# A four-stage transformer block on one core: the merged projection Wq^T Wk moves from a first stage of its own into the tail of the routing and the start of the experts, in plain float32

## The chip, the cores and the metric

The kernel runs on one core of a Trainium2 chip. The metric is the device time of one execution in microseconds. Engines are named as in the profile: PE is TensorE (matmuls; PEld its weight loads), DVE VectorE, ACT ScalarE, POOL GpSimd, SP SyncE, which here only issues DMA transfers. TensorE's clock has two levels, 1.2 and 2.4 GHz; the profile gives the granted share of the full one (0.50 or 1.00).

## What is computed

Batch B = 8, length L = 256, width D = 1024, so 16 row tiles of 128. Four residual stages (cut to what matters):

```python
x = x + tanh(g_xattn[0]) * autocorrelation(layernorm(x), ctx, ctx)   # lag attention: spectra by DFT matmuls, top 11 lags
x = x + tanh(g_ffn[0])   * moe(layernorm(x), gate_w, u, g, d)        # 16 experts, top 2, inner width 112
# third stage
Q = einsum('btx,dx->btd', layernorm(x), Wq) + bq
K = einsum('bpx,dx->bpd', ctx, Wk) + bk
x = x + tanh(g_xattn[1]) * softmax(Q K^T / 32) ctx
x = x + tanh(g_ffn[1])   * int8_style_ffn(layernorm(x))              # gate, up, down, hidden 512
```

Scores of the third stage are made as x (Wq^T Wk) ctx^T plus terms with the biases: `M` = Wq^T Wk is the merged projection (1024 x 1024), `shift` = Wk^T bq, `key_bias` = Wq^T bk, `constant` = bq.bk.

## The kernel before, in words

The program is a row of functions, one block of all engines each, with a barrier between two blocks: `merge_projections`, `lag_attention`, `route`, `experts`, `context_attention`, `quantised_ffn`. X, all 16 tiles, stays in SBUF. Each engine runs its instructions in the order written; semaphores tie them.

- `merge_projections` (names `mp_`): Wq and Wk arrive a 512 KB row block at a time. ACT makes the high part in F32R, DVE the low part, and PE makes M in 16 blocks of 128 x 512, 8 steps over k each, by `split_product` (three F32R matmuls, L44 to L46). M's parts go to DRAM (`merged`). X is loaded behind the weights, and `RowScale` makes the first layernorm's scale and shift for all tiles at once.
- `lag_attention` (`la_`): 16 units (batch b, half h of the width), software-pipelined over three steps. PE runs plain float32 products with the Fourier tables (`full_product`, L52; the trace shows each as two records). Each unit: spectra of v, of q, of v again, `positions` of the unit before, turned weights, `correlate`, `weight_spectra`. In the steps in which a batch ends, DVE also makes the next layernorm's statistics (`running_ln`: `BatchScale.variance` and `.tables`, with one `pow` on POOL). PE's third spectrum waits for ACT's copies (L253), which wait for DVE's `o_products` (L373).
- `route` (`rt_`): ACT normalises tile t into a ring of four (`rt_xn`, L677), SP stores it (`normal`), PE turns it (L766) and makes logits (L785), ACT and DVE copy it. ACT's write of tile t waits until the store of tile t-4 has landed. Then comes a DVE chain (top 2, counts, ranks, slots, ending with `place`, L758), with two PE sums in it (L790, L791). POOL loads M's parts (8 MB, L669) when all logits are there.
- `experts` (`ex_`): POOL writes the token lists by 32 indirect DMAs (L871), SP reads the list back, fills unused rows of `produced` with zeros (10 x 512 KB here), POOL gathers the first tile (`ex_xr`), and PE turns it (L949) and runs 39 tiles of gate/up (L963) and down (L975).
- `context_attention` (`xa_`): POOL gathers expert rows (two per tile, L1219 to L1222), DVE adds them to X (L1328), layernorm of batch 0 with POOL's `pow` (L564), then PE runs 8 `a_block`s per batch with M's two parts as stationary operands.

## Time and profile before

| | us |
|---|---|
| runs | 1636.74, 1643.25, 1646.53 |
| median | 1643.25 |
| profiled execution, its own time | 1643.94 |
| its span in the trace | 1642.2 |
| PE busy | 1346.5 (82%) |
| DVE busy | 794.9 (48%) |
| ACT busy | 534.8 (33%) |
| POOL busy | 424.0 (26%) |

Times in the rows below are microseconds from the start of the span. In a timeline row come start, duration, engine, line, operation, output<-input, count, and in brackets how long the engine was idle before it and what ended that. A row with a count above one spans several instructions.

### The profile page before, as it was taken

Reading aid. Unit: us, or ns where it says so; the run is one execution under the profiler, and the core shown is the slowest. Engines: PE = TensorE matmul, PEld = TensorE weight load, DVE = VectorE, ACT = ScalarE, POOL = GpSimd, SP = SyncE. Lnnn points to the kernel's source line nnn. Section 1 sums busy time; section 2 is a strip of 40 time slices with the busy share of each in tenths; the row PEclk is TensorE's granted clock in tenths of the full one; section 3 lists DMA queues with packets and bytes.
Section 4 is the critical chain, followed back from the end, with each engine's and each line's share of the span. In section 5 each row is a group of like instructions: output and inputs, shape, how many; then the busy total and the mean of one; then the engine's idle time right before and its main releaser. Section 6 shows DMA issues by size and latency. Waiting matters only on the chain. (4 is left out here: it accounts for less than half of the span.)

```text
span 1642.2 us, 20159 instructions
## 1 busy us (share of the span) xinstructions
PE 1346.5 (82%) x6217; PEld 914.8 (56%) x6217; DVE 794.9 (48%) x2134; ACT 534.8 (33%) x841; POOL 424.0 (26%) x501
## 2 busy tenths in 40 slices
PE   7896999999999976703888888829999999927876
PEld 6663444545445444603666666619888888714443
DVE  3163676786777763410222222234444443226896
ACT  3112322232232212301334333412222222147884
POOL 0130232232222321053111111232111110026785
PEclk9998999999999997855999998959999999968999
DMA  5742000000000002564666666443333321050111
GB/s 179 294 141 84 26 13 26 13 13 25 13 26 13 0 1 92 220 201 180 195 195 220 219 218 207 154 145 112 103 103 102 102 77 52 26 188 36 64 51 77
DMA packets 59426, 172.78 MB, mean 105 GB/s; under 512 B 7792, under 2 KB 15984, under 8 KB 59248
## 3 DMA queue, kind: packets, MB, share of 16 engines
q1 hardware_dynamic: 41152, 117.06, 20.1%
q0 software_dynamic: 18224, 55.08, 11.0%
q8 instruction: 29, 0.48, 0.1%
q14 instruction: 21, 0.17, 0.0%
HBM read 121.21 MB, written 50.90 MB: 105 GB/s over the span
## 5 line engine op out<-in xcount | busy, mean ns | idle before, releaser
L44 PE MATMUL xa_bank<-xa_xT_hi,M_hi 128*128 128x256 f32 x512 | 153.3, 299 | 0.0
L46 PE MATMUL xa_bank<-xa_xT_hi,M_lo 128*128 128x256 f32 x512 | 143.8, 281 | 0.0
L45 PE MATMUL xa_bank<-xa_xT_lo,M_hi 128*128 128x256 f32 x512 | 143.8, 281 | 0.0
L52 PE MATMUL la_bank<-la_v_raw,la_tab 128*128 128x512 f32 x256 | 118.5, 606 | 25.6 <-ACT la_v_spec L253 12.9
L963 PEld LDWEIGHTS ex_bank<-ex_gu,ex_xT 128*128 128x128 f32 x624 | 123.9, 201 | 25.6 <-issue 24.1
L963 PE MATMUL ex_bank<-ex_gu,ex_xT 128*128 128x224 f32 x624 | 132.8, 368 | 1.3 <-issue 1.3
L217 POOL TENSOR_TENSOR la_osum<-la_oprod 128x512 f32<-128x512 f32 x64 | 82.8, 1314 | 192.9 <-DVE la_oprod L373 192.9
L52 PE MATMUL la_bank<-la_osum,la_tab 128*128 128x512 f32 x256 | 116.3, 608 | 13.8 <-POOL la_osum L217 13.8
L949 PE MATMUL ex_bank<-ex_ident,ex_xr 128*128 128x128 f32 x320 | 45.5, 288 | 95.1 <-DMA ex_xr<-normal,ex_current 95.1
L52 PE MATMUL la_bank<-la_wT,la_tab 128*128 128x512 f32 x256 | 112.6, 593 | 1.2 <-ACT la_wT L274 1.2
L52 PEld LDWEIGHTS la_bank<-la_v_raw,la_tab 128*128 128x128 f32 x256 | 48.0, 193 | 92.3 <-issue 67.7
L1287 ACT ACTIVATE xa_A<-xa_bank,shift 128x256 f32<-128x256 f32 x64 | 30.3, 473 | 208.9 <-PE xa_bank L46 208.9
L975 PE MATMUL ex_bank<-ex_dn,ex_hT 112*128 112x512 f32 x156 | 86.3, 680 | 14.3 <-ACT ex_hT L913 14.3
L44 PEld LDWEIGHTS xa_bank<-xa_xT_hi,M_hi 128*128 128x128 f32 x512 | 96.5, 188 | 2.8 <-issue 1.7
L45 PEld LDWEIGHTS xa_bank<-xa_xT_lo,M_hi 128*128 128x128 f32 x512 | 96.6, 189 | 2.5 <-issue 1.7
L373 DVE TENSOR_TENSOR la_oprod<-la_bank,la_v_spec 128x512 f32<-128x512 f32 x128 | 80.1, 685 | 34.6 <-issue 23.4
L46 PEld LDWEIGHTS xa_bank<-xa_xT_hi,M_lo 128*128 128x128 f32 x512 | 96.4, 188 | 0.0
L949 PEld LDWEIGHTS ex_bank<-ex_ident,ex_xr 128*128 128x128 f32 x320 | 36.6, 145 | 104.7 <-issue 71.1
L52 PEld LDWEIGHTS la_bank<-la_osum,la_tab 128*128 128x128 f32 x256 | 49.9, 196 | 77.9 <-issue 62.4
L52 PEld LDWEIGHTS la_bank<-la_wT,la_tab 128*128 128x128 f32 x256 | 48.6, 190 | 55.8 <-issue 53.6
L940 DVE COPY ex_y<-ex_bank 128x512 f32<-128x512 f32 x39 | 27.0, 691 | 106.1 <-ACT ex_y L916 106.1
L929 DVE COPY ex_xT<-ex_bank 128x512 f32<-128x512 f32 x40 | 27.7, 691 | 96.6 <-PE ex_bank L949 96.6
(280 smaller groups left out, 2767.2 us busy)
## 6 DMA issues: line engine op xcount, KB each, us to landing
produced<-ex_y SPq DMA_DIRECT2D x39, 512.0 KB, 3.0
ex_gu<-in_gate_up SPq DMA_DIRECT2D x16, 896.0 KB, 6.2
X<-in_x SPq DMA_DIRECT2D x8, 1024.0 KB, 12.9
la_v_raw<-in_ctx SPq DMA_DIRECT2D x16, 512.0 KB, 3.8
normal<-rt_xn SPq DMA_DIRECT2D x16, 512.0 KB, 2.7
xa_fT<-in_ctx_T SPq DMA_DIRECT2D x8, 1024.0 KB, 5.6
xa_f<-in_ctx SPq DMA_DIRECT2D x8, 1024.0 KB, 5.0
result<-qf_final SPq DMA_DIRECT2D x16, 512.0 KB, 2.6
```

What stands on the lines that cost most here:

```text
L44: pe.matmul(out, a[0], b[0], start=first, stop=False)
L45: pe.matmul(out, a[0], b[1], start=False, stop=False)
L46: return pe.matmul(out, a[1], b[0], start=False, stop=last)
L52: return pe.matmul(out, a, b, start=first, stop=last)
L217: pool.tensor_tensor(osum[:, i, :], oprod[:, a, :], oprod[:, a + 1, :], ALU.add if i % 2 == 0 else ALU.subtract).then_inc(s["osums"], 1)
L373: dve.tensor_tensor(oprod[:, 2 * (i % 2) + k, :], bank[bk][:], vs[:, h, vk, :], ALU.mult).then_inc(s["oprods"], 1)
L929: dve.tensor_copy(xT[:, 4:8, :].rearrange("p a b -> p (a b)"), bank[3][:]).then_inc(s["xT_dve"], 1)
L940: dve.tensor_copy(y[:, 512:1024], bank[5][:]).then_inc(s["y_dve"], 1)
L949: m = pe.transpose(bank[2 + k // 4][:, (k % 4) * P:(k % 4 + 1) * P], xr[:, k * P:(k + 1) * P], ident[:])
L963: m = pe.matmul(bank[0][:, 0:UP_COLS], xT[:, k, :], gu[:, slot, k * UP_COLS:(k + 1) * UP_COLS], start=(k == 0), stop=(k == KD - 1))
L975: m = pe.matmul(bank[4 + i][:], hT[:], dn[:, slot, i * 512:(i + 1) * 512], start=True, stop=True)
L1287: act.activation(A[:, m % AHEAD, :], bank[2 + m % 2][:, 0:L], ACT.Identity, bias=shift[:, m:m + 1]).then_inc(s["a_out"], 1)
```

## The change

`merge_projections` is gone. `lag_attention` comes first: SP loads X batch by batch between the context loads, and DVE makes the first layernorm per batch (`BatchScale`, as for the second), batch b+2 at the end of each step with h = 1. During lag attention SP also zeroes tiles 32 to 47 of `produced` and loads Wk whole. `route` loads Wq whole after its eighth store, and PE makes M there in plain float32 by `merged_product` (8 `matmul`s of 128 x 512 a block): 4 of the 16 blocks in `route` after the logits, 12 at the start of `experts` ahead of the first turn. The bias vectors are made by DVE (`weigh`, sums weighted by the bias) and 17 PE products of one column. `context_attention` makes the parts: ACT the high one (8 copies), POOL the low one (8 subtractions between its gathers).

```diff
@@ lag_attention, SP
+            load_x(0)
             load_v(0, 0, 0)
+            sp.dma_start(tab[:], tables).then_inc(s["tab_in"], 16)
+            sp.dma_start(graw[:], column(gate, 0)).then_inc(s["gate_in"], 16)
             load_v(1, 0, 1)
-            with sp.Fori(1, B) as b:
+            load_x(1)
+            load_x(2)
...
+            with sp.Fori(1, B - 2) as b:
                 for h in range(2):
                     load_v(2 * b + h, b, h)
+                    fill(2 * b + (FEWEST - 2 + h))
+                load_x(b + 2)
+            sp.dma_start(Wk_home[:], Wk.rearrange("(k p) n -> p k n", p=P)).then_inc(s["Wk_in"], 16)
@@ lag_attention, ACT and DVE
+                act.wait_ge(norm.ready, b + 1)
...
+                if due is not None:
+                    dve.wait_ge(x_in, 16 * (due + 1))
+                    norm.variance(dve, X, due)
+                    norm.tables(dve, due)
+            dve.wait_ge(x_in, 16)
+            norm.variance(dve, X, 0)
+            norm.tables(dve, 0)
             steps(dve, step)
@@
+EARLY = 4
+SUMS_AT = 1
+def merged_product(pe, out, W, n):
+
+    for k in range(KD):
+        last = pe.matmul(out, W[1][:, k, (n // 2) * P:(n // 2 + 1) * P], W[0][:, k, (n % 2) * 512:(n % 2 + 1) * 512],
+                         start=(k == 0), stop=(k == KD - 1))
+    return last
@@ route, SP
             for t in range(TILES):
+                if t == TILES // 2:
+                    sp.dma_start(W[1][:], Wq.rearrange("(k p) n -> p k n", p=P)).then_inc(s["wq_in"], 16)
                 sp.wait_ge(s["xn_ready"], t + 1)
@@ route, POOL
-            pool.wait_ge(s["logits"], TILES)
-            for part in range(2):
-                pool.dma_start(M[part][:], merged[part].rearrange("(k p) n -> p k n", p=P)).then_inc(m_in, 16)
@@ route, DVE
             for t in range(TILES):
+                if t >= TILES - KD:
+                    weigh(0, t - (TILES - KD))
...
             dve.tensor_tensor(place[:], place[:], place_tile[:], ALU.add).then_inc(s["placed"], 1)
+            dve.wait_ge(s["wq_in"], 16)
+            for k in range(KD):
+                weigh(1, k)
+            dve.wait_ge(s["columns"], 1)
@@ route, PE
+            for n in range(EARLY):
+                if n == SUMS_AT:
+                    sums()
+                at_least(pe, s["m_out"], n - 3)
+                merged_product(pe, bank[n % 4][:], W, n).then_inc(s["m_pe"], 1)
+            pe.wait_ge(s["by_bias"], 2 * KD)
...
@@ experts, PE
+            for n in range(EARLY, 2 * KD):
+                at_least(pe, s["m_out"], n - EARLY - 3)
+                merged_product(pe, bank[merged_bank[n % 4]][:], W, n).then_inc(s["m_pe"], 1)
...
@@ experts, SP
-            with sp.Fori(total, MAX_TILES + 1) as g:
-                row = sp.snap(g * P)
-                sp.dma_start(produced[bass.ds(row, P), :], zeros[:]).then_inc(s["filled"], 16)
@@ context_attention, POOL
+            merged_low(0)
             gather(0, 2)
+            merged_low(1)
             gather(0, 3)
+            merged_low(2)
             gather(1, 0)
...
@@ context_attention, ACT
+            for m in range(KD):
+                part = (slice(None), slice(None), slice(m * P, (m + 1) * P))
+                act.activation(M[0][part], M32[part], ACT.Copy).then_inc(s["m_hi"], 1)
             act.wait_ge(s["gate_in"], 32)
```

PE, from the last logits (L785 before, L840 after) to the first turned expert tile: before.

```order
L785 MATMUL rt_bank<-rt_gw,rt_xnT 128x16 x7
L790 MATMUL rt_bank<-rt_both,rt_ones 128x256 [waits la_v_ev1]
L791 MATMUL rt_bank<-rt_both,rt_before 128x256
L605 UNCONDITIONAL_BRANCH
L942 UNCONDITIONAL_BRANCH [waits barrier_Pool_Activation_PE_DVE_SP_release]
L949 MATMUL ex_bank<-ex_ident,ex_xr 128x128 [waits la_top_chain,la_oprods]
```

The same place after the change; L602 is `merged_product`, L821 and L822 the two sums, L855 and L856 the bias columns.

```order
L840 MATMUL rt_bank<-rt_gw,rt_xnT 128x16 x7
L602 MATMUL rt_bank<-Wk,Wq 128x512 [waits la_corr_sb,la_filled,la_zeroed]
L602 MATMUL rt_bank<-Wk,Wq 128x512 x7
L821 MATMUL rt_bank<-rt_both,rt_ones 128x256 [waits la_q_ready]
L822 MATMUL rt_bank<-rt_both,rt_before 128x256
L602 MATMUL rt_bank<-Wk,Wq 128x512 x24
L855 MATMUL rt_bank<-rt_ones,rt_by_bias 128x1 [waits la_maxed,la_exed]
L855 MATMUL rt_bank<-rt_ones,rt_by_bias 128x1 x15
L856 MATMUL rt_bank<-rt_b_sum,rt_ones 128x1
L614 UNCONDITIONAL_BRANCH
L1001 UNCONDITIONAL_BRANCH [waits barrier_Pool_Activation_PE_DVE_SP_release]
L602 MATMUL ex_bank<-Wk,Wq 128x512 [waits la_achain]
```

After that last row PE has 95 more matmuls of L602 before it turns the first tile: one block stands ahead of the sums, three behind them, twelve behind the barrier. (Semaphores keep the number, and so the name, of an earlier block here.)

POOL at the start of `context_attention` after the change; L1145 is `merged_low`, L1128 to L1131 a gather, L555 the `pow` of the layernorm of batch 0.

```order
L1145 TENSOR_TENSOR M_lo<-M_2476,M_hi 128x8x128 [waits xa_m_hi]
L1128 TENSOR_TENSOR xa_small_u<-slots,xa_small_u 128x1 [waits xa_combined]
L1130 TENSOR_TENSOR xa_small_u<-xa_small_u 128x1 [waits xa_at]
L1131 DMA xa_got<-produced,xa_small_u 128x1024
...
L1145 TENSOR_TENSOR M_lo<-M_2476,M_hi 128x8x128 [waits xa_m_hi]
L555 TENSOR_TENSOR ln_small<-ln_small 128x2 [waits xa_ln_var_ready,xa_ln_power_set]
```

Before, the gathers and the `pow` followed each other with nothing between; now five of the eight subtractions stand ahead of the `pow` (the rows shown are the first subtraction, the first gather behind it, and the fifth subtraction with the `pow`; three more pairs of a subtraction and a gather lie between).

SP in `route` after the change: the weights' 4 MB stand between the eighth and the ninth store, on the same queue.

```order
L663 DMA token_of<-rt_no_token 128x50 [waits la_v_ev2]
L668 DMA normal<-rt_xn 128x1024 [waits la_dchain] x8
L666 DMA Wq<-in_Wq 128x8x1024
L668 DMA normal<-rt_xn 128x1024 [waits la_dchain] x8
L614 UNCONDITIONAL_BRANCH [waits la_out_pe,la_top_chain,la_osums,la_oprods]
```

Before, all 16 stores stood in one row (L649).

## Rows read from the trace of the kernel before

**Rows 1.** Busy time in stretches: start:end, length, busy of each engine, PEclk, DMA share, GB/s.

```profile
340.00:360.00 20.00, 20.00 (x62) 10.90 (x61) 14.44 (x48) 4.26 (x8) 4.65 (x5) 1.00 0.07 25
...
766.00:770.00 4.00, 4.00 (x11) 3.60 (x12) 0.00 (x0) 0.58 (x1) 0.17 (x1) 0.50 0.98 373
```

**Rows 2.** Timeline by engine, from the start to lag attention's first products.

```profile
0.83 0.40 SPq L1016 DMA_DIRECT2D mp_b_raw<-in_bq  x1
...
125.98 0.34 SPq L179 DMA_DIRECT2D la_tab<-in_tables  x1
...
126.05 0.07 DVE L305 MEMSET la_nextv<- 128x8 f32 x1 [0.34 <-PEq L986]
...
135.32 0.20 ACT L234 ACTIVATE la_tg<-la_graw 128x1 f32<-128x1 f32 x1 [9.82 <-DMA la_graw<-in_g_xattn]
135.43 1.50 ACT L242 ACTIVATE la_q_n<-X,first_ln_shift,first_ln_scale 128x512 f32<-128x512 f32 x2
...
142.05 3.60 PE L52 MATMUL la_bank<-la_q_n,la_tab 128*128 128x512 f32 x8
```

**Rows 3.** Timeline of DVE, lag attention, a step with a layernorm.

```profile
347.00 0.06 DVE L569 MEMSET running_ln_small<- 128x2 f32 x1
...
352.05 0.43 DVE L337 MAX8 la_top<-la_corr 128x8 f32<-128x256 f32 x1
...
357.19 2.48 DVE L373 TENSOR_TENSOR la_oprod<-la_bank,la_v_spec 128x512 f32<-128x512 f32 x4
```

**Rows 4.** Timeline of PE, lag attention, 300 to 368 us and 600 to 645 us.

```profile
305.40 3.70 PE L52 MATMUL la_bank<-la_v_raw,la_tab 128*128 128x512 f32 x8 [1.21 <-ACT la_v_spec L253]
308.94 7.03 PE L52 MATMUL la_bank<-la_osum,la_tab 128*128 128x512 f32 x16
...
334.75 3.70 PE L52 MATMUL la_bank<-la_v_raw,la_tab 128*128 128x512 f32 x8 [0.71 <-ACT la_v_spec L253]
...
625.50 8.61 PE L52 MATMUL la_bank<-la_osum,la_tab 128*128 128x512 f32 x16 [6.75 <-POOL la_osum L217]
```

**Rows 5.** Timeline of the routing, by engine.

```profile
655.58 1.23 ACT L677 ACTIVATE rt_xn<-X,running_ln_shift,running_ln_scale 128x1024 f32<-128x1024 f32 x1
...
667.05 1.23 ACT L677 ACTIVATE rt_xn<-X,running_ln_shift,running_ln_scale 128x1024 f32<-128x1024 f32 x1
...
679.93 4.35 PE L785 MATMUL rt_bank<-rt_gw,rt_xnT 128*128 128x16 f32 x34
...
704.04 0.19 DVE L758 CUSTOM_DVE_ANT_0 place<-place,rt_place_tile 128x64 uint16<-128x64 uint16 x1
...
709.47 0.20 POOL L864 MEMSET ex_ident<- 128x128 f32 x1 [22.71 <-POOLq L605]
```

**Rows 6.** DMA issues, 685 to 765 us: KB each, median us from issue to landing.

```profile
M_hi<-merged POOLq DMA_DIRECT2D x1, 4096.0 KB, 14.0
```

**Rows 7.** Timeline of the experts' start, by engine.

```profile
749.82 0.97 POOL L871 DMA_INDIRECT token_of<-token,place  x1 [0.30 <-issue]
...
762.57 1.94 PE L949 MATMUL ex_bank<-ex_ident,ex_xr 128*128 128x128 f32 x8 [70.43 <-DMA ex_xr<-normal,ex_current]
...
775.26 3.19 PE L963 MATMUL ex_bank<-ex_gu,ex_xT 128*128 128x224 f32 x16
...
781.73 3.23 PE L963 MATMUL ex_bank<-ex_gu,ex_xT 128*128 128x224 f32 x16
```

**Rows 8.** Timeline of context attention's start.

```profile
1084.92 0.19 POOL L1219 TENSOR_TENSOR xa_small_u<-slots,xa_small_u 128x1 uint32<-128x1 uint32 x1 [1.02 <-DVE X L1328]
...
1094.22 0.72 POOL L564 TENSOR_TENSOR ln_small<-ln_small 128x2 f32<-128x2 f32 x1 [1.55 <-DVE ln_small L581]
...
1102.95 2.67 DVE L1328 SCALAR_TENSOR_TENSOR X<-xa_got,weights,X 128x1024 f32<-128x1024 f32 x2
...
1104.57 1.09 POOL L1221 TENSOR_TENSOR xa_small_u<-xa_small_u 128x1 uint32<-128x1 uint32 x1
```

**Rows 9.** Groups by line of POOL, whole span: count, busy us, mean ns.

```profile
L1600 POOL TENSOR_TENSOR qf_final<-qf_y,X 128x1024 f32<-128x1024 f32 x16 | 37.7, 2354 | 11.0 <-DVE qf_y L1673 11.0
```

More of the change, by code:

```diff
@@ L167, in on @@
                     return u + off, b + (h + off) // 2, (h + off) % 2
-                step(on)
+                step(on, b + 2 if h == 1 and not (isinstance(b, int) and b + 2 >= B) else None)
             for u in range(-2, 2):
                 one(u, u // 2, u % 2)
-            with eng.Fori(1, B - 1) as b:
+            with eng.Fori(1, B - 2) as b:
                 one(2 * b, b, 0)
                 one(2 * b + 1, b, 1)
-            for u in range(U - 2, U + 1):
+            for u in range(U - 4, U + 1):
                 one(u, u // 2, u % 2)
@@ L636, in route @@
         no_token = sb("no_token", [P, ROW_TILES], I32)
-        names = "gw_in consts turned xnT_act xnT_dve logits one xn_ready chain sums_pe slots_ready ex_ready gap_ready no_token no_list placed".split()
+        b_raw = sb("b_raw", [P, 2, KD])
+        bb = sb("bb", [P, KD])
+        b_sum = sb("b_sum", [P, 1])
+        by_bias = sb("by_bias", [P, 2, D])
+        key_sum = sb("key_sum", [P, KD])
+        names = "gw_in consts turned xnT_act xnT_dve logits one xn_ready chain sums_pe slots_ready ex_ready gap_ready no_token no_list placed b_in wq_in dot by_bias columns key_sum key_hi m_pe m_out".split()
         s = {n: sem(n) for n in names}
-        stored = [sem(f"stored{i}") for i in range(4)]
+        stored = [sem(f"stored{i}") for i in range(RING)]
         block = ctx.enter_context(nc.Block())
@@ L766, in turn, with sums @@
                 return pe.transpose(bank[2 * (t % 2) + k // 4][:, (k % 4) * P:(k % 4 + 1) * P],
-                                    xn[:, t % 4, k * P:(k + 1) * P], ident[:])
+                                    xn[:, t % RING, k * P:(k + 1) * P], ident[:])
+            def sums():
+                pe.wait_ge(s["chain"], 6)
+                flat = both[:].rearrange("p t e -> p (t e)")
+                pe.matmul(bank[5][:, 0:TILES * EXPERTS], ones[:], flat, start=True, stop=True)
+                pe.matmul(bank[6][:, 0:TILES * EXPERTS], before[:], flat, start=True, stop=True).then_inc(s["sums_pe"], 1)
             for t in range(2):
@@ L787, in _, with experts @@
                 m.then_inc(s["logits"], 1)
-            pe.wait_ge(s["chain"], 6)
-            flat = both[:].rearrange("p t e -> p (t e)")
-            pe.matmul(bank[5][:, 0:TILES * EXPERTS], ones[:], flat, start=True, stop=True)
-            pe.matmul(bank[6][:, 0:TILES * EXPERTS], before[:], flat, start=True, stop=True).then_inc(s["sums_pe"], 1)
-def experts(nc, gate_up, down, normal, token_of, token, place, produced, first_tile):
+            pe.wait_ge(s["xnT_act"], TILES)
+            pe.wait_ge(s["xnT_dve"], TILES)
+            pe.wait_ge(s["wq_in"], 16)
+            for n in range(EARLY):
+                if n == SUMS_AT:
[3 more added lines that the diff above has]
+            pe.wait_ge(s["by_bias"], 2 * KD)
+            pe.wait_ge(s["dot"], 2)
+            for v in range(2):
+                for i in range(KD):
+                    pe.matmul(bank[7][:, v * KD + i:v * KD + i + 1], by_bias[:, v, i * P:(i + 1) * P], ones[:, 0:1], start=True, stop=True)
+            pe.matmul(bank[7][:, 2 * KD:2 * KD + 1], ones[:], b_sum[:], start=True, stop=True).then_inc(s["columns"], 1)
+def experts(nc, gate_up, down, normal, token_of, token, place, produced, first_tile, W, M32):
     with ExitStack() as ctx:
@@ L951, in turn @@
                         m.then_inc(s["turned"], 1)
+            for n in range(EARLY, 2 * KD):
+                at_least(pe, s["m_out"], n - EARLY - 3)
+                merged_product(pe, bank[merged_bank[n % 4]][:], W, n).then_inc(s["m_pe"], 1)
+            pe.wait_ge(s["m_out"], 2 * KD - EARLY)
             turn(0)
@@ L1136, in context_attention @@
-def context_attention(nc, produced, slots, weights, ffn_gate, features, features_T, M, m_in, shift, key_bias, constant, gate, X,
+def context_attention(nc, produced, slots, weights, ffn_gate, features, features_T, M32, M, shift, key_bias, constant, gate, X,
                       after):
@@ L1765, in build, with with_guest @@
         running = BatchScale(nc, stack, "running_ln")
[L1766 to L1775 removed]
+        with ExitStack() as projection:
+            def with_guest(name, guest):
+                at = -(-nc.sbuf_base // 32) * 32
+                owner = projection.enter_context(nc.sbuf_tensor(name, [P, KD, D], F32R))
+                return owner, nc.alloc_sbuf_tensor_at(guest, [P, KD, D], F32, offset=at)
+            M_hi, Wk_home = with_guest("M_hi", "Wk")
+            lag_attention(nc, x, ctx, g_xattn, tables, Wk, Wk_home, X, running, produced)
+            M_lo, M32 = with_guest("M_lo", "M32")
+            slots = projection.enter_context(nc.sbuf_tensor("slots", [P, TILES, 2], U32))
+            weights = projection.enter_context(nc.sbuf_tensor("weights", [P, TILES, 2], F32))
+            first_tile = projection.enter_context(nc.sbuf_tensor("first_tile", [P, EXPERTS + 1], I32))
             with ExitStack() as lists:
```

318 lines of the change are left out of this document (96 added, 222 removed).

## The prediction

> **What bounds the kernel now.** I read the stretches first. In lag attention PE is busy all 20 us of a stretch at a granted clock of 1.00 and DVE 14.4 of them [rows 1]. Then I read the timelines where PE does not work: before the first Fourier product of q at 142.05, which the merged projection and the loads of lag attention precede [rows 2], and from the end of the logits at 684.3 [rows 5] to the first turned expert tile at 762.57, where PE sat idle for 70.4 us [rows 7]. The change takes work out of the first place and puts it into the second, so the end of the kernel moves by what is saved at 142.05 less what comes later. In between, the chain is: lag attention on PE, a DVE chain in the routing, POOL's list writing, PE's experts, context attention on PE.
>
> **The start.** The work before lag attention goes. What stays is its own entry: before, the table's transfer was issued at 125.98 and the gate value, behind the table, was used at 135.32, 9.3 us later [rows 2]. Now the first transfer issues at about 0.83 [rows 2], and 1.57 MB more (a batch of X, half a batch of the context) stand ahead of the gate. 4.19 MB took 14.0 us to land [rows 6], 0.30 MB per us, so 1.57 MB is 5.2 us: the gate is there at 15.4. DVE waits for the tanh of it before its first layernorm, which takes 5.05 us (347.00 to 352.05, [rows 3]); two copies of q take 1.5 [rows 2]. With 0.3 for hand-overs q's product starts at 22.2 in place of 142.05: **-119.9**. PE does the first spectra of v meanwhile, as before. Bounds: the 1.57 MB hidden beside the other loads, -125; twice as slow, -115.
>
> **Lag attention.** DVE gets seven more layernorms (batches 1 to 7), each at the end of a step with h = 1, which had none. Steps that end with a layernorm are in the trace: PE then waits 1.21 us for ACT's L253, in the others 0.71 [rows 4]. So one costs 0.5 us, not 5.05; DVE's idle 5.6 us in 20 [rows 1] hides the rest. **+3.5**. Bounds 0 and 35 (all of it). The X loads, the zeroing and Wk's 4 MB lie in a stage whose DMA share is 0.07 [rows 1]; if PE did not cover them, Wk alone would cost 14 us, but no load of v is issued within a unit of it.
>
> **Wq in the routing.** Tile 7 is ready at 656.8 (655.58 + 1.23); Wq is issued right behind its store, on the same queue, and 4 MB need about 14 us [rows 5, 6], so it ends near 669 to 671. The store of tile 8 is behind it, some 1.5 us more. ACT's write of tile 12 waits for that store; it started at 667.05 [rows 5]. It is 3.5 to 5.5 us late, and the copy of tile 10, PE's turns and all later tiles queue behind it on ACT. **+4.5**. Bounds: 0, if the queue interleaves; +8, if PE also loses its clock.
>
> **The tail of the routing and the experts' start.** 16 records of 512 columns take 7.03 us at full clock [rows 4]; a merged block is 8 such products, 16 records, so with overlap 6.9 us. Times here leave out the 4.5 us. Logits end at 684.28 (679.93 + 4.35, [rows 5]). Block 0 ends at 691.2, a little after DVE has made its counts, which takes it some 6 us from the logits; the two sums then run at full clock and not at half, so DVE gets them when it did, and `place` ends at 704.23 as before [rows 5]. Blocks 1 to 3 end at 712.8. DVE goes on with 8 weighted sums of 1024 columns; the nearest row is L1328, 2.67 us for two [rows 8], so 10.7 us: 714.9. The other 8 sums lie in DVE's gaps between tiles (a tile takes 11.47 / 5 = 2.29 us [rows 5], of which DVE has one copy of 512 columns to make, under 1.3; 1.33 more fits barely, at worst 0.3 a tile). PE's 17 one-column products are 34 records; the last two tiles' logits are 34 records too and took 4.35 us [rows 5]: 719.3. Copies and the change of block take 1.8 us (0.34 at the change to lag attention [rows 2]; up to 5 if it goes as at 704.2 to 709.47 [rows 5], where I think M's 8 MB on POOL's queue held it: issued at the end of the logits, with 14.0 us for the first half [rows 6]): 721.1. Twelve blocks at 6.9 are 83 us, and the first run below full clock: after an idle 6.75 us 16 records took 8.61 in place of 7.03 [rows 4], 1.6 us. PE turns the first tile at 805.7 in place of 762.57: +43.1. POOL's 32 list writes end 41 us after its block began (709.47 to 750.8, [rows 5, 7]), then list and gather some 12 us more (to 762.57, shorter without the zero fill): 721 + 53 = 774, under PE's 83 us. The 4 MB loads of M and the 5 MB fill lay beside that idle time and free nothing. PE is warm at the first tile: 762.57 to 775.26 took 12.7 us with the granted clock at 0.50 [rows 1, 7]; at full clock a turn and copies of 2.3 and one tile of 6.5 (775.26 to 781.73) make 8.8, -3.9. Together **+39.2**.
>
> **Context attention.** POOL's subtraction of 1024 columns is nearest L1600, 2.35 us [rows 9]. Gather (0, 3), at 1084.92 [rows 8], now stands behind two subtractions and gather (0, 2): it starts at 86.3; then subtraction, gather (about 1.6, from its three instructions on POOL), subtraction, gather, subtraction end at 98.15, and only then comes the `pow`, at 1094.22 before [rows 8]: +3.9. ACT's 8 copies (at most 1.23 each, L677's time, 9.8 in all [rows 5]) end about when the first gathered rows land; I add 0.6. PE's first `a_block`s come behind the turn and the bias row, some 12 us after the `pow`, when six of the parts are there; the last two are made while PE runs the first. **+4.5**; bounds 0 and +9.
>
> A row bears on this: POOL's L1221, otherwise 0.19 us, took 1.09 at 1104.57, while DVE's L1328 ran from 1102.95 to 1105.62 [rows 8]. The Trainium skill, "SBUF — State Buffer", section "SBUF: two separate sides", says that GpSimd and a DVE operation with two SBUF inputs take the shared port pair in turn, each for a whole instruction. By that rule the subtractions ahead of the `pow` would each wait for a combine that runs, and the sum would be some 3 us more; the trace agrees for that one instruction.
>
> **Sum.** -119.9 + 3.5 + 4.5 + 39.2 + 4.5 = -68.2. From the profiled execution's 1643.94 that is 1575.7; the median lies 0.7 lower, so **1575**.
>
> **Rivals.** (A) The stores are not held by Wq: 1571. For it: transfers of one queue overlap at their ends; against: the gate value of some bytes took 9.3 us behind the table [rows 2]. (B) Each subtraction on POOL waits for a running combine of DVE, 1.3 us each, for two or three ahead of the `pow`: 1578. (C) DVE becomes lag attention's bound: its layernorms cost all of their 5.05 us, 7 times, +32 beyond mine: 1607. For it: `o_products` start at 357.19, directly behind the lags of a step that was late [rows 3], so the slack is used up; against: PE's wait shows only 0.5 [rows 4]. It decides if DVE does not catch up within a step. (D) A float32 product from these tiles costs one record, 0.43 us: the twelve blocks take 41 us, POOL's lists end last at about 774, 1575 - 32 = 1543. Against: all L52 products show two. (E) The other side: PE runs the blocks at the low clock of 1.2 GHz. Twelve blocks are 83 us more, the early ones some 20: 1575 + 103 = 1678. It is slower than before as soon as two thirds of the blocks' time is at the low level. Against: lag attention kept PE busy without a gap at 1.00 [rows 1].
>
> **Chances and range.** My sum with its stall 0.55, A 0.17, B 0.12, C 0.06, D 0.03, E 0.03, something unseen 0.04. Low end: A, and no cost in context attention and at the cold start, with 2 us off the start: 1562. High end: Wq 8, a block change of 5, one-column products half as slow again, 3 for the start, 3 for POOL: 1593. A measurement of this kernel can tell about 0.5%, 8 us. All but E and part of the unseen are faster by more: 0.96; within 0.5% 0.01; slower 0.03.
>
> **What would show it.** q's first product near 22; PE waits of 1.2 at L253 in every step; a gap of PE in the routing near tile 10; PE busy from the block change for 83 us and the first turn some 43 us later than the routing's shift alone gives; the `pow` of batch 0 some 4 us later after the experts' end. Wrong would make it above all a list or gather chain longer than 83 us, a clock that falls in the blocks, or a dearer step in lag attention.

## The result, and the profile of the changed kernel

The changed kernel takes 1592.3 us, median of 4 runs (1590.1 to 1598.1); the kernel before took 1641.4 in the same rounds. The ratio is 0.971, 95% interval 0.968 to 0.974. Run again twice beside later experiments it gave 0.975 (0.971 to 0.980) and 0.974 (0.971 to 0.977). So it is faster, by 40 to 49 us where 68 were forecast. On the forecast's own base, 1643.25, the ratio gives 1595.8, above the range of 1562 to 1593. The profiled execution spans 1596.4 us, 45.8 less than the one of before.

I first set both traces beside each other at eight marks, each the start of one row of the timeline. All lengths are us. The last three columns are experiments of the next section; "again" is the changed kernel in a second profiled execution.

| from ... to ... | before | changed | again | wq_spread | dve_low | best |
|---|---|---|---|---|---|---|
| start, q's first product | 142.1 | 22.0 | 20.1 | 21.4 | 21.6 | 17.8 |
| ... routing's first transfer | 499.3 | 507.1 | 504.1 | 507.2 | 507.4 | 502.8 |
| ... DVE's copy of the logits | 43.0 | 56.9 | 57.0 | 43.2 | 56.9 | 43.0 |
| ... experts' first transfer | 25.2 | 38.0 | 38.0 | 38.0 | 38.0 | 38.1 |
| ... first turned expert tile | 53.0 | 94.7 | 94.6 | 95.1 | 95.2 | 86.1 |
| ... context attention's first transfer | 309.0 | 298.3 | 298.5 | 302.9 | 306.8 | 302.3 |
| ... its first turn on PE | 25.9 | 36.9 | 37.1 | 37.1 | 28.4 | 28.9 |
| ... the end | 544.8 | 542.4 | 545.3 | 544.2 | 545.3 | 543.4 |

The start and the routing's tail came as forecast; the third, fifth and seventh lines are each dearer than forecast by 6.5 to 10 us. The timeline of the start (start and length in us, engine, line, operation, count; in brackets the idle time ahead and what ended it) answers to [rows 2]:

```profile
12.39 5.45 PE L52 MATMUL la_bank<-la_v_raw,la_tab 128*128 128x512 f32 x8 [12.39 <-DMA la_tab<-in_tables]
14.74 0.20 ACT L265 ACTIVATE la_tg<-la_graw 128x1 f32<-128x1 f32 x1 [12.63 <-DMA la_graw<-in_g_xattn]
15.06 0.69 DVE L564 BATCH_NORM_STATS2 first_ln_stats<-X 128x6 f32<-128x512 f32 x1 [14.11 <-ACT la_tg L265]
...
21.98 5.40 PE L52 MATMUL la_bank<-la_q_n,la_tab 128*128 128x512 f32 x8 [4.15 <-ACT la_q_n L274]
```

The gate is there at 14.7, DVE starts on it and q's product comes at 21.98. Its first 8 records take 5.40 us where 8 took 3.60 before [rows 2]: PE had waited 4.15 us and the clock was low.

The timeline of the routing, SP's queue and ACT, answers to [rows 5]:

```profile
544.04 0.44 SPq L666 DMA_DIRECT2D Wq<-in_Wq  x1
...
553.40 0.60 ACT L704 ACTIVATE rt_xnT<-rt_bank 128x512 f32<-128x512 f32 x1 [0.57 <-PE rt_bank L840]
560.14 1.24 ACT L693 ACTIVATE rt_xn<-X,running_ln_shift,running_ln_scale 128x1024 f32<-128x1024 f32 x1 [6.14 <-DMA normal<-rt_xn]
...
566.46 0.60 ACT L704 ACTIVATE rt_xnT<-rt_bank 128x512 f32<-128x512 f32 x1 [1.85 <-PE rt_bank L840]
...
570.72 0.60 ACT L704 ACTIVATE rt_xnT<-rt_bank 128x512 f32<-128x512 f32 x1 [2.54 <-PE rt_bank L840]
```

Wq goes out behind the eighth store, and ACT's normalise of tile 12 waits 6.14 us for the store that stands behind it. This is the stall of the forecast. But the copies after it come every 4.27 us and not every 2.29. The windows of the same stretch (PE busy first, then PEld, DVE, ACT, POOL, the granted clock, the DMA share and GB/s) say why:

```profile
550.00:555.00 5.00, 5.00 (x55) 5.00 (x54) 3.65 (x5) 2.86 (x4) 0.00 (x0) 1.00 1.02 415
555.00:560.00 5.00, 2.89 (x31) 2.79 (x29) 4.06 (x5) 0.00 (x0) 0.00 (x0) 0.87 1.00 357
560.00:565.00 5.00, 3.09 (x18) 3.09 (x19) 0.00 (x0) 4.46 (x5) 0.00 (x0) 0.50 1.01 414
565.00:570.00 5.00, 5.00 (x31) 5.00 (x30) 1.88 (x2) 1.73 (x2) 0.00 (x0) 0.50 0.50 197
570.00:575.00 5.00, 5.00 (x30) 5.00 (x30) 1.89 (x3) 0.61 (x2) 0.00 (x0) 0.50 0.07 27
575.00:580.00 5.00, 5.00 (x29) 5.00 (x29) 2.58 (x3) 1.18 (x2) 0.00 (x0) 0.50 0.00 0
580.00:585.00 5.00, 5.00 (x26) 5.00 (x25) 0.00 (x0) 0.00 (x0) 0.00 (x0) 0.50 0.01 2
...
590.00:595.00 5.00, 5.00 (x14) 2.32 (x14) 2.16 (x11) 0.48 (x2) 0.00 (x0) 1.00 0.00 0
```

PE stands still for 4.0 us, the clock falls to its lower level (0.50, 1.2 of 2.4 GHz), and it stays there for over 20 us although PE is busy all the time, with 30 records in 5 us where it had 55. It rises in the first merged block. At the start of the stage it had risen: PE began at 531.45, behind 9.7 us without work, with 17 turns in a row, and the granted clock was 0.50 from 532 to 534, 0.81 from 534 to 536 and 1.00 from 536 us on. Why it does not rise again behind the stall is open.

The timeline of the experts' start, PE, ACT and POOL, answers to [rows 7]:

```profile
624.58 38.73 PE L602 MATMUL ex_bank<-Wk,Wq 128*128 128x512 f32 x83 [1.72 <-POOL ex_ident L923]
...
641.46 0.60 ACT L965 ACTIVATE M<-ex_bank 128x512 f32<-128x512 f32 x1 [6.27 <-PE ex_bank L602]
...
653.89 0.60 ACT L965 ACTIVATE M<-ex_bank 128x512 f32<-128x512 f32 x1 [11.84 <-DMA la_v_raw<-in_ctx]
...
663.68 0.59 PE L602 MATMUL ex_bank<-Wk,Wq 128*128 128x512 f32 x1 [0.37 <-issue]
664.20 0.96 POOL L928 DMA_INDIRECT token_of<-token,place  x1 [0.30 <-issue]
666.48 0.59 PE L602 MATMUL ex_bank<-Wk,Wq 128*128 128x512 f32 x1 [2.21 <-issue]
669.28 31.21 PE L602 MATMUL ex_bank<-Wk,Wq 128*128 128x512 f32 x66 [2.21 <-issue]
...
671.49 1.08 ACT L965 ACTIVATE M<-ex_bank 128x512 f32<-128x512 f32 x2 [16.99 <-DMA la_v_raw<-in_ctx]
```

A block takes 6.87 us. ACT makes the copy of the third 5.6 us late and that of the fourth 16 us late, though PE had finished both; and PE, which waits for nothing, stops twice for 2.21 us; behind the stops the granted clock is 0.50 for another 5.4 us. POOL's row is the last of its 32 list writes. (The transfer named at ACT's waits is none of this stage; none of that tensor is issued here.)

The timeline of context attention's start, answering to [rows 8]:

```profile
1035.91 5.37 DVE L1253 SCALAR_TENSOR_TENSOR X<-xa_got,weights,X 128x1024 f32<-128x1024 f32 x2 [4.58 <-DMA xa_got<-produced,xa_small_u]
1036.44 2.35 POOL L1145 TENSOR_TENSOR M_lo<-M,M_hi 128x1024 fp32r<-128x1024 f32 x1
...
1048.65 0.73 POOL L555 TENSOR_TENSOR ln_small<-ln_small 128x2 f32<-128x2 f32 x1
1049.36 2.33 POOL L1145 TENSOR_TENSOR M_lo<-M,M_hi 128x1024 fp32r<-128x1024 f32 x1
1049.41 2.30 DVE L577 TENSOR_TENSOR ln_small<-ln_small 128x2 f32<-128x2 f32 x1 [4.56 <-POOL ln_small L555]
1051.75 0.16 DVE L579 TENSOR_TENSOR ln_small<-ln_small 128x2 f32<-128x2 f32 x1
...
1054.00 3.40 PE L1333 MATMUL xa_bank<-xa_ident,xa_xn 128*128 128x128 f32 x16 [46.30 <-ACT xa_xn L1197]
```

Two combines of DVE take 5.37 us beside a subtraction, where two took 2.67 [rows 8] (one of them 3.98 us, the other 1.29), and a step of two elements takes 2.30 and not 0.16. The first combine, with no subtraction beside it, starts 11.6 us into the stage and not 9.4: POOL's first gather goes out 2.1 us later than before, behind 1.95 us in which POOL waits for nothing that the profile shows (0.16 before).

### The profile page after: what moved, and what is told of

Its sections match the earlier page's. It is cut to its first block and busy times, and to the rows that moved or that the text cites. A ratio compares the mean times of both kernels' runs of the same rounds, so it can differ in the third digit from the quotient of the medians.

```text
span 1596.4 us, 19695 instructions
## 1 busy us (share of the span) xinstructions
PE 1360.1 (85%) x6035; PEld 894.1 (56%) x6041; DVE 797.0 (50%) x2181; ACT 523.3 (33%) x827; POOL 428.1 (27%) x481
## 3 DMA queue, kind: packets, MB, share of 16 engines
q1 hardware_dynamic: 41792, 120.20, 21.4%
## 5 line engine op out<-in xcount | busy, mean ns | idle before, releaser
L52 PE MATMUL la_bank<-la_v_raw,la_tab 128*128 128x512 f32 x256 | 118.5, 606 | 29.5 <-ACT la_v_spec L285 16.3
L1026 PEld LDWEIGHTS ex_bank<-ex_gu,ex_xT 128*128 128x128 f32 x624 | 119.6, 194 | 22.4 <-issue 20.9
L52 PE MATMUL la_bank<-la_osum,la_tab 128*128 128x512 f32 x256 | 117.4, 613 | 13.8 <-POOL la_osum L246 13.8
L1026 PE MATMUL ex_bank<-ex_gu,ex_xT 128*128 128x224 f32 x624 | 127.3, 358 | 0.7 <-ACT ex_xT L961 0.7
L1038 PE MATMUL ex_bank<-ex_dn,ex_silu_then_turned 112*128 112x512 f32 x156 | 83.1, 658 | 14.3 <-ACT ex_silu_then_turned L973 14.3
L602 PE MATMUL ex_bank<-Wk,Wq 128*128 128x512 f32 x192 | 88.7, 624 | 6.5 <-issue 4.8
L933 POOL TENSOR_TENSOR ex_current<-ex_listed,ex_nought 128x1 int32<-128x1 int32 x41 | 7.7, 188 | 271.6 <-PE ex_bank L1008 268.6
```

The source lines that it names most:

```text
L52: return pe.matmul(out, a, b, start=first, stop=last)
L602: last = pe.matmul(out, W[1][:, k, (n // 2) * P:(n // 2 + 1) * P], W[0][:, k, (n % 2) * 512:(n % 2 + 1) * 512], start=(k == 0), stop=(k == ...
L1026: m = pe.matmul(bank[0][:, 0:UP_COLS], xT[:, k, :], gu[:, slot, k * UP_COLS:(k + 1) * UP_COLS], start=(k == 0), stop=(k == KD - 1))
L1038: m = pe.matmul(bank[4 + i][:], hT, dn[:, slot, i * 512:(i + 1) * 512], start=True, stop=True)
```

## Experiments

All are edits of the changed kernel. Times are medians, with their range; each set ran beside the kernel before, 1641 to 1645. The whole time of the changed kernel spreads by some 20 us from run to run, so the stage's own length in the profile decides where a few us are at stake.

**1. The stores held by Wq.**

```
-                if t == TILES // 2:
-                    sp.dma_start(W[1][:], Wq.rearrange("(k p) n -> p k n", p=P)).then_inc(s["wq_in"], 16)
+                if t % 2 == 0:
+                    sp.dma_start(W[1][:, t // 2, :], Wq[t // 2 * P:(t // 2 + 1) * P, :]).then_inc(s["wq_in"], 16)
```

> Wq is loaded as eight pieces of 0.5 MB, one ahead of each second store, in place of 4 MB behind the eighth. Theory (the 4 MB hold the store that the normalise of tile 12 waits for, PE stands still for 4.0 us and then works at a granted clock of 0.50, 4.27 us a tile in place of 2.29): the stall and the slow tiles both go, from the routing's first transfer to the copy of the logits 43 us as before the change and not 57, the kernel 12 to 14 us under the changed one, near 1579. Rival 1 (DVE's eight weighted sums of Wk, which the change also put among these tiles, slow the tiles): the tiles stay at 4.27 us, the kernel gains at most the 4 us of the stall. Rival 2 (the clock would have fallen in this stage whatever the stall, as the engine does many small records): as rival 1, with the clock at 0.50.

1590.4 (1580.6 to 1592.6), ratio 0.967 (0.964 to 0.970). The stage took 43.2 us. Two windows of wq_spread, and two rows of DVE's timeline in it:

```profile
555.00:560.00 5.00, 5.00 (x55) 5.00 (x55) 3.96 (x5) 3.66 (x5) 0.00 (x0) 1.00 1.07 401
560.00:565.00 5.00, 5.00 (x55) 5.00 (x55) 4.18 (x5) 2.72 (x4) 0.00 (x0) 1.00 0.80 323
```

```profile
562.71 1.28 DVE L729 SCALAR_TENSOR_TENSOR rt_by_bias<-Wk,rt_b_raw,rt_by_bias 128x1024 f32<-128x1024 f32 x1
564.39 0.69 DVE L737 COPY rt_xnT<-rt_bank 128x512 f32<-128x512 f32 x1 [0.41 <-PE rt_bank L840]
```

No gap, clock 1.00, a tile in 2.29 us. DVE's weighted sum fits beside its copy with 0.41 us to spare in the same stage, so rival 1 falls; the clock stays at 1.00 through all the tiles, so rival 2 falls. (It falls only at the very end, in the 34 records of 16 columns behind the last turn: 0.68 from 568 to 569 us and 0.50 from there. Before the change it fell there too, to 0.57 from 683 to 684 us.) The whole 14 us were the one held store: 4 us of it a gap, 10 us the clock behind it. The stage shows this; the time of the whole kernel, 1590 and not the 1579 expected, does not: the intervals of its ratio and of the changed kernel's overlap. In the profiled execution 4.6 of the 13.8 us are lost again in the experts' tiles.

**2. POOL's subtractions: five places for them.** The first kernel puts all eight behind the `pow`:

```
             gather(0, 2)
             gather(0, 3)
             gather(1, 0)
             gather(1, 1)
             norm.on_pool(pool, 0)
+            for m in range(4):
+                merged_low(m)
             gather(1, 2)
+            merged_low(4)
+            merged_low(5)
             gather(1, 3)
+            merged_low(6)
+            merged_low(7)
```

> In context attention POOL makes the four gathers it needs and the pow of batch 0 first, and the eight subtractions of the merged matrix behind them. Theory (POOL's five subtractions ahead of the pow cost the start of this stage 11.0 us: they delay the gathers, and DVE's operations with two inputs stand still while one runs): from the stage's first transfer to PE's first turn 26 to 28 us in place of 36.9, and some 2 us of it given back where DVE makes the low halves of the rows beside the subtractions; the kernel 7 to 10 us under the changed one. Rival (the subtractions were needed anyway before the first product, and DVE and POOL only meet later): the turn comes earlier but PE waits for the low half of the matrix instead, the kernel within 2 us.

1603.4 (1598.1 to 1609.4), 0.977 (0.974 to 0.980): no faster than the changed kernel, and the first turn comes after 37.0 us as there. My theory had the right mechanism and the wrong result. Timeline of pow_first:

```profile
1040.99 9.22 POOL L1145 TENSOR_TENSOR M_lo<-M,M_hi 128x1024 fp32r<-128x1024 f32 x4
1041.04 2.30 DVE L577 TENSOR_TENSOR ln_small<-ln_small 128x2 f32<-128x2 f32 x1 [0.91 <-POOL ln_small L555]
1043.38 2.27 DVE L579 TENSOR_TENSOR ln_small<-ln_small 128x2 f32<-128x2 f32 x1
1045.68 2.27 DVE L581 TENSOR_SCALAR ln_small<-ln_small 128x2 f32<-128x2 f32 x1
1047.98 2.25 DVE L583 TENSOR_TENSOR ln_small<-ln_small 128x2 f32<-128x2 f32 x1
```

The `pow` is 6.3 us earlier in the stage (25.3 us into it, 31.6 in the changed kernel). But four steps of two elements are now held by a subtraction each, where one was in the changed kernel, and the three more take 2.1 us each: the 6.3 us are gone again. So the next kernel adds `pool.wait_ge(norm.ready, 1)` ahead of the first subtraction, and one more also moves ACT's eight copies behind the gates.

> As pow_first, and POOL waits until DVE has the scale and shift of batch 0 before the first subtraction. Theory (a subtraction of 2.3 us on POOL holds up each two-input operation of DVE; in pow_first four of them stood beside DVE's four small steps between the pow and the scale, 2.27 us each and not 0.16, which gave back all that the earlier pow had won): the small steps take 0.16 us again, the scale is there 1.1 us behind the pow, PE turns the first rows 27 to 29 us after the stage's first transfer in place of 36.9; the subtractions lie beside PE's turn and bias row; the kernel 6 to 9 us under the changed one. Rival (the eight subtractions then come too late for PE's blocks, or hold DVE's low halves of the rows): PE waits for M_lo or xT_lo, 4 us or less won.

> As low_after_scale, and ACT makes its eight copies of the merged matrix (7.7 us) behind the gates and the row of ones, not ahead of them. Theory (the copies cost this stage 2 us more than they should: POOL's first gather starts 1.6 us later than before the change though it waits for nothing): the first gather comes 0.8 us after the stage's first transfer again and the first combine 9.4 us in place of 11.6, PE turns another 1 to 2 us earlier, some 26 us after the first transfer. Rival (the late gather has to do with the stage's change, not with ACT's copies): no difference from low_after_scale.

1597.6 (1592.8 to 1599.6), 0.973 (0.969 to 0.978), and 1595.8, 0.972 (0.966 to 0.978). The first turn comes after 28.9 us in low_after_scale, as expected, and after 28.7 in low_late, where 26 were expected. But from there to the end it is 550.3 and 548.8 us instead of 542 to 545: gather (1, 2) stands behind four subtractions, the layernorm of batch 1 is late, and PE waits 5.37 us (low_after_scale) for a copy queued on ACT. In low_late POOL's first gather still starts 2 us late (1.99 idle), so ACT's copies are not its cause and the rival holds. What the cause is stays open.

> As low_after_scale, but the subtractions are laid between the gathers: one, gather (1, 2), two, gather (1, 3), five. low_after_scale had PE turn the first rows 28.9 us after the stage's first transfer in place of 36.9 but gave 6 of the 8 us back: gather (1, 2) stood behind four subtractions, the layernorm of batch 1 and ACT's normalise came late, and PE stood still for 5.4 us for a copy of A that was queued behind it on ACT. Theory: with the gathers earlier this wait goes, the first turn stays at 28.9, and context attention keeps 6 to 8 us. Rival (the subtractions take POOL's and DVE's time wherever they stand, some 19 us in all, and batch 1 is late by it): PE waits again for 3 us or more at 1065 to 1075.

1594.4 (1592.6 to 1598.5), 0.970 (0.967 to 0.974). The rival holds: 28.9 us to the turn, then 548.0, with a wait of 4.0 us on PE. Timeline of low_spread:

```profile
1056.20 11.78 POOL L1145 TENSOR_TENSOR M_lo<-M,M_hi 128x1024 fp32r<-128x1024 f32 x5
1059.57 9.49 DVE L1251 SCALAR_TENSOR_TENSOR X<-xa_got,weights,X 128x1024 f32<-128x1024 f32 x1 [4.56 <-DMA xa_got<-produced,xa_small_u]
```

A combine of 1.28 us stands until five subtractions in a row are done. Last, DVE makes them itself, first thing in the stage, and POOL's eight go:

```
+            for m in range(KD):
+                part = (slice(None), slice(None), slice(m * P, (m + 1) * P))
+                dve.wait_ge(s["m_hi"], m + 1)
+                dve.tensor_tensor(M[1][part], M32[part], M[0][part].bitcast(F32), ALU.subtract).then_inc(s["m_lo"], 1)
             dve.wait_ge(s["tg_done"], 2)
```

> DVE makes all eight low halves of the merged matrix, first thing in context attention, in step with ACT's copies; POOL only gathers and makes the pow, in the order of the kernel before the change. In low_spread five subtractions in a row on POOL held one combine of DVE for 9.5 us, where it takes 1.3. Theory (the price is POOL beside DVE, and DVE waits for its first gathered rows anyway until 11.6 us into the stage): eight at 1.3 us are done at 11 us, the first turn of PE comes 27 to 29 us after the stage's first transfer in place of 37, and nothing is given back: 542 to 545 us from there to the end of the kernel (548 in low_spread, 549 in low_late); 8 to 10 us under the changed kernel. Rival (the eight subtractions cost their time on either engine): the turn at 33 us or later.

1590.4 (1588.5 to 1601.3), 0.968 (0.965 to 0.971), 9 us under the changed kernel in the same rounds. 28.4 us to the turn and 545.3 from there. Timeline of dve_low:

```profile
1027.05 9.27 DVE L1232 TENSOR_TENSOR M_lo<-M,M_hi 128x1024 fp32r<-128x1024 f32 x8 [8.81 <-ACT M_hi L1168]
...
1037.17 1.28 DVE L1244 SCALAR_TENSOR_TENSOR X<-xa_got,weights,X 128x1024 f32<-128x1024 f32 x1 [0.65 <-DMA xa_got<-produced,xa_small_u]
```

The same eight subtractions cost 9.27 us of time in which DVE had nothing to do. The price was POOL beside DVE, not the work. The 2.5 us that are left against the kernel before (28.4 and 25.9) are the late first gather for the most part: the first combine starts 11.2 us into the stage and not 9.4.

**3. The gaps in the twelve blocks.** First 4 of the 32 list writes (`for t in range(2)`; most expert rows are then token 0), and twice the same products from half the code:

```
+            for first, count in ((2, 4), (6, 2)):
+                with pe.Fori(0, 2) as h:
+                    for i in range(count):
+                        pe.wait_ge(s["m_out"], 4 * h + i + (1 if first == 2 else 9))
+                        for k in range(KD):
+                            last = pe.matmul(bank[merged_bank[i]][:], W[1][:, k, (first + i) * P:(first + i + 1) * P],
+                                             W[0][:, k, bass.ds(h * 512, 512)], start=(k == 0), stop=(k == KD - 1))
```

> POOL writes 4 of the 32 token lists and leaves 28 out, so most expert rows are token 0; the work of every engine is otherwise the same. Theory (instruction fetches of PE and ACT are held up behind the list writes: ACT copies blocks 2 and 3 some 5 and 16 us late, PE stands still for 4.8 us near 665 though it waits for nothing): without them the copies come every 6.9 us from the second block on and no gap is seen; from the block's start to the last copy 85 to 87 us in place of 93.5. Rival (the code of the blocks or the experts' weight loads make the gap): the gap and 93.5 stay.

> The twelve blocks of the merged product in the experts' stage are written as two loops over the two halves of 512 columns, on PE and on ACT, so half as much code does the same products (in another order). Theory (PE and ACT run out of fetched instructions while POOL writes its 32 lists, 41 us): the first turn of the loop needs only 32 of the 96 products as new code in 28 us and the second none, so the two gaps of 2.2 us on PE and ACT's late copies shrink or go; from the block's start to the last copy 85 to 89 us in place of 93.5, the kernel 4 to 8 us under the changed one. Rival (the list writes slow the engines in another way, for example their reads of memory): the gaps stay, 93 us.

four_lists: 1585.8, 0.965 (0.961 to 0.970), which leaves work out. The gaps are gone. PE's timeline of four_lists:

```profile
620.57 84.31 PE L602 MATMUL ex_bank<-Wk,Wq 128*128 128x512 f32 x192 [1.72 <-POOL ex_ident L923]
705.57 1.10 PE L1008 MATMUL ex_bank<-ex_ident,ex_xr 128*128 128x128 f32 x8 [0.69 <-ACT M L965]
```

loop: 1602.7 (1601.9 to 1607.2), 0.976 (0.971 to 0.981). The gaps stay, at the same place: PE stops after 79 records of 192 (83 in the changed kernel) in the last microseconds of the list writes, and the stage takes 96.4 us. So half the code does not help, and my expectation was wrong in that; its rival, that the list writes slow the engines in another way, came true in its number. One turn of the loop is 64 records, so PE stops in the second turn, whose products are no new code. PE's timeline of loop:

```profile
622.73 35.67 PE L1020 MATMUL ex_bank<-Wk,Wq 128*128 x79 [2.01 <-POOL ex_ident L923]
658.60 0.59 PE L1020 MATMUL ex_bank<-Wk,Wq 128*128 x1 [0.20 <-issue]
660.71 0.59 PE L1020 MATMUL ex_bank<-Wk,Wq 128*128 x1 [1.53 <-issue]
```

The next kernel keeps all code and all lists and only spaces them: `at_least(pool, s["m_pe"], t // 2)` ahead of each pair.

> POOL writes four lists and then waits for the next block of the merged product, so that it pauses some 1.8 us in each 6.9 and is done near 680 and not 665. The loop run has shown that half the code does not help: PE stopped at the same product, the fortieth. Theory 1 (PE and ACT cannot get new instructions while POOL issues indirect transfers without a pause): in the pauses they get them, ACT's copies come at most 7 us late and PE shows no gap; 85 to 87 us from the block's start to the last copy. Theory 2 (they get none until all the lists are written): PE stops after its fortieth product until some 680, a gap of 17 us, 103 us or more in all. Rival (the list writes have no part in it): gaps as now, 93.5.

1597.8 in two runs, 0.972 (0.968 to 0.976). The stage takes 86.7 us and shows no gap, as theory 1 has it. That the pauses are used to fetch instructions is not shown by it. The whole time can't be told from the changed kernel's, 0.975 in the same rounds. Timeline of paced:

```profile
622.98 85.46 PE L602 MATMUL ex_bank<-Wk,Wq 128*128 128x512 f32 x192 [1.73 <-POOL ex_ident L923]
...
636.98 0.96 POOL L929 DMA_INDIRECT token_of<-token,place  x1 [0.30 <-issue]
...
646.68 0.60 ACT L966 ACTIVATE M<-ex_bank 128x512 f32<-128x512 f32 x1 [6.27 <-PE ex_bank L602]
653.54 0.60 ACT L966 ACTIVATE M<-ex_bank 128x512 f32<-128x512 f32 x1 [6.27 <-PE ex_bank L602]
```

**4. Lag attention and the start.** one_first_ln makes the layernorm ahead of q for batch 0 alone and uses its scale for all; gate_first issues `graw` ahead of x.

> The layernorm ahead of q is made for batch 0 alone and its scale and shift are used for all batches; the seven running ones of DVE and POOL are left out. Theory (of the 7.8 us by which lag attention grew, 4 to 5 are PE's longer waits where a layernorm ends DVE's step, the rest is the low clock in its first and last products): the routing's first transfer comes 4 to 5 us after the first product of q less than in the changed kernel, 502.5 us behind it in place of 507.1. Rival 1 (the X loads and the zero fill beside it cost the time): 507 stays. Rival 2 (layernorm costs it all): 499.

> The transfer of the gate value is the first one on the queue, ahead of x, the context and the table. Theory (q's first product waits for DVE's layernorm, which waits for the tanh of the gate behind three large transfers, 15.1 us): DVE starts when the first batch of x has landed, at 7 to 10 us, q's product starts near 15 to 17 in place of 22, and the kernel ends 4 to 7 us earlier. Rival (the table, on which PE waits, is no earlier and x is no earlier either): DVE starts at 13 or later, 2 us or less.

one_first_ln: 499.1 us from q's first product to the routing, the 499.3 of before, where 502.5 were expected. Its whole time, 1600.8, says nothing, since other scales sent the tokens to 40 expert tiles and not 39. Without it the kernel shows 502.8 (low_spread) to 507.4 (dve_low) in this stretch, so the seven layernorms cost 3.7 us, and the other 0 to 4.5 depend on the execution. PE's waits for ACT say the same: its 14 waits of 60 to 480 us (L285) add up to 16.3 us in the changed kernel, and the same 14 to 12.9 before the change (L253, 180 to 600 us). As to the rest: where the first q spectra take 5.40 us (changed, dve_low) and not 3.70 (again, low_spread), the clock is low in three places, at q's spectra, the first correlation and the last positions, and 4 us are lost against low_spread. gate_first: 1596.5, 0.972 (0.966 to 0.979). DVE starts at 6.86, a little before the 7 to 10 expected, but q's product comes only at 18.5 and not at 15 to 17, since PE now has the spectra of v in front of it: 3.5 us before the changed kernel's first profile, 1.6 before its second.

**5. The changed kernel again, and the edits together.**

> The changed kernel once more, on the chip and in the rounds of the next three runs, so that they have a time to stand beside: 1590 to 1598. Between the marks of its profile (q's first product, the routing's first transfer, the logits' copy, the experts' first transfer, the first turned expert tile, context attention's first transfer, its first turn) 503 to 507, 57, 38, 93 to 95, 298 to 303 and 37 us, as in the runs so far, where a stage that no edit touched repeated within 1 us but for lag attention and the experts' tiles.

> The edits of wq_spread, low_spread and gate_first together. If each keeps what its stage showed: 14 us in the routing, 6 to 8 in context attention and 2 to 3 at the start, some 23 us under the changed kernel in the same rounds, near 1571, 0.957 of the kernel before. If what one stage wins is lost again to the clock in the experts' tiles (298 to 303 us in the runs so far, with no edit there), 15 to 20.

> The changed kernel once more in the rounds of the next three: 1590 to 1605, its stages as in after_again.

> The edits of wq_spread, gate_first and dve_low together: 14, 2 and 9 us, 25 under the changed kernel in these rounds; 1573, as combined or 3 to 7 us under it.

> As best_unpaced, and the list writes paced as in paced. If the 7 us of the gaps reach the end: 1566, 7 under best_unpaced. Rival (the experts' tiles behind run at a lower granted clock when PE had no pause, 307 us in paced where the changed kernel had 298): within 3 us of best_unpaced, with a longer stage of experts' tiles.

after_again 1604.7 (1586.9 to 1609.7), after_third 1599.5 (1590.9 to 1608.1). combined 1580.3 (1570.3 to 1585.8), 0.960 (0.956 to 0.963), 24 us under the changed kernel of its rounds, as expected. best_unpaced 1578.8 (1575.9 to 1582.2), 0.961 (0.958 to 0.963), is 21 us under it where 25 were expected, no better than combined; best 1564.1 (1560.9 to 1568.5), **0.952 (0.950 to 0.955)**, 35 us under the changed kernel and 15 under best_unpaced, where 7 were expected. Timeline of best:

```profile
602.27 84.87 PE L602 MATMUL ex_bank<-Wk,Wq 128*128 128x512 f32 x192 [1.72 <-POOL ex_ident L923]
687.82 1.09 PE L1009 MATMUL ex_bank<-ex_ident,ex_xr 128*128 128x128 f32 x8 [0.69 <-ACT M L966]
```

Pacing alone is worth 8.7 us there (94.8 to 86.1 in this stage), so its rival, that the experts' tiles give it back, does not hold: 302.3 us against 304.2. The medians differ by 15; the rest of that I can't place. The experts' tiles, in which no edit was made, took from 297 to 307 us over all profiled executions of the changed kernel and its edits with 39 tiles and all lists, in no order that follows the edits; that is as much as most of the edits are worth. It is not the only spread: the three profiled executions of the changed kernel, 1589.2 to 1596.4, took 297.4 to 298.5 there, but 502.9 to 507.1 in lag attention.

## Why the prediction was off, step by step

- **The start, -119.9**: right. Gate 14.7 (forecast 15.4), q 21.98 (22.2), -120.1.
- **Lag attention, +3.5**: the layernorms cost 3.7, as forecast, and rival C (they cost all) is out. The profiled execution shows +7.8, as the clock falls at q's spectra; "Bounds 0 and 35" named only DVE and left the clock out.
- **Wq in the routing, "+4.5 ... Bounds: 0 ... +8, if PE also loses its clock"**: this step failed, by 9.5 us. The stall was where I put it and 4 to 6 us long. But the lost clock stood only in the bound, at 3.5 us, and without a working; the one loss that I did work out, at the blocks, was 1.6 us behind the gap of 6.75 us of [rows 4]. Here it cost 10, because the clock stayed at 0.50 for the rest of the stage, from 561.9 to 585.8 us. **+14.0**. wq_spread takes 13.8 of this away.
- **Tail and experts' start**: from the logits to the experts +12.8 (forecast +11.6), right within the change of block. The twelve blocks: +41.7 against +31.6. "Twelve blocks at 6.9 are 83" is right as a price (84.3 in four_lists with a cold start of some 2), and a list chain shorter than that is right too (the list arrives at 668.3). What I had not seen is that 32 list writes without a pause stop PE and ACT: 8 to 9 us here (this length was 92.3 to 96.4 us in all profiled executions with unpaced writes, 85.6 to 86.7 with four or paced ones). This is the largest failed step, by 10.1 us: I had the list writes lie beside PE's blocks at no cost. Before the change both were idle in that time [rows 7], so no row could show it. The first tile came 9.9 us behind its turn in place of 12.7, -2.8 (forecast -3.9).
- **Context attention, +4.5, bounds 0 and 9**: measured +11.0, the third failed step, by 6.5 us. Rival B was right in kind and wrong in size. It counted two or three subtractions that wait for a combine, 1.3 us each. The dearer waits fell on the other side, on DVE: one combine took 3.98 us and not 1.28, and one small step 2.30 and not 0.16, 4.8 us together. Another 2.2 are the late first gather, for which the forecast had no term and whose cause no run shows. The rule that I cited, from the Trainium skill, "SBUF — State Buffer", section "SBUF: two separate sides", says that either engine blocks the other for a whole instruction; the traces agree (0.16 becomes 2.30 beside a POOL operation of 2.33), and low_spread goes past it: one DVE operation was held through several in a row, 9.49 us.
- **Given back**: the experts' tiles took 10.7 us less than before and the end 2.4 less, of which I forecast 3.9. In the experts' tiles it is the clock: granted 0.96 where it was 0.92, PE busy 248.6 us where it was 259.5, with the same number of records. The warm first tile is 2.8 us of it. Whether the change has a part in the rest is not shown: the only profiled execution of before took 309.0, and no profiled execution of a changed kernel took that long.

In all: -68.2 forecast; +4.3 lag attention, +9.5 Wq, +1.2 and +10.1 at the experts' start, +6.5 context attention, -6.8 and -2.4 behind make, but for rounding, -45.8, the difference of the spans. The high end of the range added Wq at 8, a longer block change and small sums, but nothing for blocks that stop, for lag attention or for more than 3 us on POOL; that all went the same way is why it missed. (Its own terms add up to 1590 and not 1593.) That the tiles and the end gave back 9.2 us more than forecast is luck. Rivals A and D fell: the stores were held, and a block is 16 records. So did E: PE ran the blocks at 1.00, but for the first block of each stage and 5.4 us behind the stops.

## What to carry to other kernels

Ask of each new transfer what stands behind it on its queue, and of each stall what PE does next: a wait of 4 us cost 14, since what followed was small matmuls at half clock. Work moved into the idle time of others is only free if that time was idle for a reason that stays: list writes that hurt nobody while PE waited for them cost 6 to 9 us once PE worked beside them, until they got pauses. And give elementwise work to DVE in its own idle time before giving it to POOL beside DVE.

## What the runs showed of the hardware

- The granted clock stayed at 0.50 for 24 us in which PE was busy throughout with turns of 128 columns and products of 16 columns, at 30 records in 5 us, and rose in products of 512 columns. At 1.00 it kept that level through the same turns and products (wq_spread), up to the last 34 products of 16 columns, in which it fell with PE busy. At the start of the stage it rose from 0.50 to 1.00 with PE at work on such records, behind 17 turns in a row. So the same records did not always get the same level.
- While POOL issued indirect transfers one behind the other, 1.26 us each, ACT and PE stopped without anything to wait for; with a pause of 2.1 us after each four (paced, best) neither did. That they lack new instructions in that time is my reading. For it: both engines stop, ACT first and at the third copy in the changed kernel and in loop, and no semaphore is late. Against it: half the code (loop) did not help, and the DMA view lists two instruction packets between 622 and 672 us in the changed kernel and two in paced, the larger at 653 and at 652 us, so none that is late. The cause stays open.
- One POOL instruction holds one DVE step: in pow_first four subtractions, 9.22 us, held four steps of two elements, 2.25 to 2.30 us each and not 0.16. Several in a row can hold a single one: in low_spread 11.78 us of five subtractions held one combine of 1.28 us for 9.49.
